# Two graph layers with a nearest-neighbour search: the squared norms of the search added by 32-row matmuls in four row groups

## The chip, the core and the metric

The kernel runs on one core of one Trainium2 chip. The metric is the device time of one execution in microseconds, the median of several runs.

## What is computed

Two graph layers act on `x` (4096 nodes of 128 features) with a dense weighted adjacency `adj` (4096 x 4096). The first layer builds node vectors `z`, finds for each node its four nearest neighbours by squared distance, and adds weights exp(-distance/2) for them to the adjacency. Cut to what matters:

```python
z  = leaky_relu(_lap_mul(A, x) @ W1 + b1, negative_slope=0.1)
sq = jnp.sum(z * z, axis=-1)
d2 = sq[:, None] + sq[None, :] - 2.0 * (z @ z.T)
S  = jnp.exp(-jnp.sqrt(jnp.maximum(d2, 0.0) + 1e-10) / (2.0 * sigma))
S  = jnp.where(ranks_of_S < 4, S, 0.0)
out = _lap_mul(S + A, x) @ W2 + b2
```

The second layer is a plain `x @ W_self.T + (adj @ x) @ W_neigh.T + b`. Both layers have a layer norm, a ReLU and a residual around them.

## The kernel before, in words

The program is written engine by engine, with semaphores by hand; each engine executes its own list in order. There are 32 tiles of 128 nodes (`TILES`), taken in 8 groups of 4 (`GROUPS`, `U`). Names on the left of `<-` in a row are what is written.

1. **Reading the adjacency** (0 to about 412 us). GpSimd issues the loads of `adj` (L365), VectorE transposes blocks of 32 (L862), ScalarE sums rows, and the transposed units go back to memory for later passes.
2. **First pass** (to about 541 us). TensorE multiplies stored units (L1157) group after group. When a group's product is complete, a chain `finish_first` of small steps turns it into z: VectorE `add_partial` (L908), TensorE L1204, VectorE `make_z` (L924 four times, L926), TensorE transposes (L1150) into the bank `ps_t`, ScalarE copies the part of z rounded to fp32r into `zt_hi` (L686) and squares it (L689), VectorE `split_z` writes the rest into `zt_lo` (L931), TensorE multiplies the squares by a matrix of -0.5 (L1217). This leaves in every row of the bank `ps_q` the same thing: minus half the squared norm of each of the group's 512 nodes. Then comes what the change touches. ScalarE copies rows 0 to 31 of `ps_q`, rounded, into `sq_rows` (L695), and rows 32 to 63, rounded, into `z_st` (L697); VectorE's `split_sq` subtracts the rounded value in rows 32 to 63 and writes the rest there (L937). So row 0 of `sq_rows` holds the high part and row 32 the low part, and `pick` (ones in rows 0 and 32, zeros elsewhere) adds the two. The lists `STAGE_A/B/C` and `MAKE_Z`, `SPLIT_SQ`, counted in tiles of the pass, set where each engine does these steps; on VectorE `split_sq` of one group stands directly ahead of `make_z` of the next.
3. **Search** (about 541 to 809 us). For each of 32 tiles, GpSimd copies the tile's columns into `zs_hi`, `zs_lo` (`stage_tile`, L492, L493); TensorE (`distances`) fills eight banks of 512 columns with four matmuls each: the norms (L1252) and the three products of high and low parts (L1253 to L1255); ScalarE (`leave`, L714) brings each pair of banks to `keys[par]`, one buffer for even tiles and one for odd. VectorE searches a pair of tiles: of the even tile only the maximum of each block of 128 (`bmax`, L975, then L977, L981), of the odd one all 4096 keys (MAX8 L988, FIND_INDEX8 L990), then the even tile's four best blocks, which GpSimd has fetched back from memory (`read_blocks`, L498 to L505), as candidates (L995, L997). `leave` of an even tile waits for `block_maxima` of the pair before and for the store of its keys (`keys_out`), of an odd one for `max_done` (L990). On GpSimd the staging of the odd tile stands behind the four fetches of `read_blocks`, and these wait for `block_places` (L981) and for `keys_out`. From tile 1 on, TensorE's matmul into an even bank waits until ScalarE has taken that pair of banks of the tile before (`key_ev`).
4. **Second and third pass** (about 809 us to the end): three matmuls per block (L1274 to L1276) over operands split on ScalarE (L731) and VectorE (L1018), with the gathers of the neighbours on GpSimd (L576) beside the second.

Of the kernel before, what the change touches and what calls it, by code (L numbers as in the profile page):

```python
# [22 lines left out]
F32 = mybir.dt.float32  # L23
# [12 lines left out]
U = 4  # L36
# [14 lines left out]
def gnn_kernel(nc, x, adj, W1, b1, W2, b2, W, b, out):  # L51
# [16 lines left out]
    with ctx:  # L68
# [538 lines left out]
        def _(act):  # L607
# [71 lines left out]
            def finish_first(k):  # L679
# [15 lines left out]
                act.activation(sq_rows_g[0:R, g], ps_q[0:R].rearrange("p (u q s) -> p u q s", u=U, q=QD), ACT.Copy).then_inc(qh_done, 1)  # L695
                act.wait_ge(sq_done, k + 1)
                act.activation(flat(z_st[R:2 * R]).bitcast(F32R), ps_q[R:2 * R], ACT.Copy).then_inc(qh_done, 1)  # L697
# [133 lines left out]
        def _(v):  # L831
# [11 lines left out]
            link(v.memset(pick[:].bitcast(F32), 0.0))  # L843
            v.memset(pick[0:1].bitcast(F32), 1.0)
            v.memset(pick[R:R + 1].bitcast(F32), 1.0)
            v.memset(sq_rows[2 * R:P].bitcast(F32), 0.0)
# [87 lines left out]
            def split_sq(k_f):  # L934
                g = F1[k_f]
                v.wait_ge(qh_done, 2 * k_f + 2)
                v.tensor_tensor(sq_rows_g[R:2 * R, g], ps_q[R:2 * R].rearrange("p (u q s) -> p u q s", u=U, q=QD),  # L937
                                z_st[R:2 * R].rearrange("p u (q s) -> p u q s", s=R), ALU.subtract).then_inc(q_done, 1)
# [198 lines left out]
        def _(pe):  # L1137
# [105 lines left out]
            def distances(it, par):  # L1243
                pe.wait_ge(zs_ready, it * 2 + 2)
                for c in range(8):
                    cols = slice(c * 512, c * 512 + 512)
                    if c % 2 == 0 and not (isinstance(it, int) and it < 1):
                        pe.wait_ge(key_ev, it * 4 + (c // 2 - 3))
                    zh = zt_hi[:].rearrange("p q t s -> p (q t s)")[:, cols]
                    zl = zt_lo[:].rearrange("p q t s -> p (q t s)")[:, cols]  # L1250
                    sq = sq_rows[:].rearrange("p q t s -> p (q t s)")[:, cols]
                    pe.matmul(ps[:, c], pick[:], sq, start=True, stop=False)  # L1252
                    pe.matmul(ps[:, c], zs_hi[:, par], zl, start=False, stop=False)  # L1253
                    pe.matmul(ps[:, c], zs_lo[:, par], zh, start=False, stop=False)  # L1254
                    ins = pe.matmul(ps[:, c], zs_hi[:, par], zh, start=False, stop=True)  # L1255
                    if c % 2:
                        ins.then_inc(bank_mm, 1)
# [110 lines left out]
```

## Time and profile before

| | us |
|---|---|
| median of 3 runs | 1305.23 |
| the three runs | 1304.32, 1305.23, 1310.51 |
| the profiled execution, its own time | 1303.21 |
| its span, first to last instruction | 1301.2 |

Mean granted TensorE clock over the span: 0.886 of full speed (full is 2.4 GHz, the lower level is half of it).

| stretch | us from the span's start |
|---|---|
| adjacency read and transposed | 0 to 412 |
| first pass | 412 to 541 |
| search | 541 to 809 |
| second and third pass | 809 to 1301 |

How to read it: a timeline row gives start, duration, engine, line, operation, what is written and read, the count, and in brackets the engine's idle time before it and what ended that. A matmul's row is longer than the distance to the next one's start, since matmuls are pipelined; the distance of two starts is what a matmul costs in a stream. PEld rows are weight loads.

### The profile page before, as it was taken

The numbers are of one execution on the slowest core, as the hardware profiler recorded it, in microseconds if no ns is written. First come the engines' busy times: TensorE is split into PE (matmuls) and PEld (weight loads), VectorE is DVE, ScalarE is ACT, GpSimd is POOL, SyncE is SP. The second block draws the span as 40 slices with busy tenths as digits, with TensorE's granted clock in tenths as the row PEclk, the third lists the DMA queues.
The fourth block names the chain that finished last, engine by engine and source line by source line (L and its number), as shares of the span: only waits on it lengthen the run. The fifth ranks groups of instructions, "written<-read, shape, count | busy, mean of one in ns | idle before, by whom it ended". The sixth has DMA issues, their size and how long they took to land.

```text
span 1301.2 us, 13552 instructions
## 1 busy us (share of the span) xinstructions
PE 934.7 (72%) x3570; PEld 664.9 (51%) x3570; DVE 888.0 (68%) x852; ACT 597.3 (46%) x1105; POOL 657.8 (51%) x936
## 2 busy tenths in 40 slices
PE   0132154474776999899999994666777777799998
PEld 0111022232333444477777773455666666588886
DVE  1966665654554321288999999937777777788885
ACT  0533343162460322255555555635555554567673
POOL 9798779877820000044444444588888887200000
PEclk9985676786987999899999998788888888899999
DMA  9999999999996975295444445695777777599993
GB/s 222 323 349 367 363 343 382 349 365 351 354 374 230 357 266 187 92 262 200 158 157 157 155 157 206 184 379 203 282 279 271 284 274 273 215 358 384 381 382 124
DMA packets 117253, 357.73 MB, mean 275 GB/s; under 512 B 34528, under 2 KB 59872, under 8 KB 89568
## 3 DMA queue, kind: packets, MB, share of 16 engines
q1 hardware_dynamic: 60896, 273.11, 55.2%
q0 software_dynamic: 47104, 80.00, 20.6%
q10 hardware_dynamic: 9216, 4.20, 1.2%
q8 instruction: 14, 0.23, 0.1%
q14 instruction: 23, 0.19, 0.0%
HBM read 250.02 MB, written 106.95 MB: 274 GB/s over the span
## 4 chain that ended last, share of the span: by engine, by line
PE 31%; POOL 21%; DMA 18%; issue 14%; DVE 11%; ACT 2%; SPq 1%; POOLq 0%; DVEq 0%; ACTq 0%
DMA araw<-in_adj_dram 15%; POOL zt_lo L576 11%; PE ps L1157 7%; POOL araw L365 7%; PE ps L1274 4%; PE ps L1275 4%; PE ps L1276 4%; PE ps L1252 2%; PE ps L1253 2%; PE ps L1254 2%; PE ps L1255 2%; DVE m L988 2%; DVE bmax L975 2%; DVE i L990 2%; POOL t_st L505 1%
## 5 line engine op out<-in xcount | busy, mean ns | idle before, releaser
L365 POOL DMA_DIRECT2D araw<-in_adj_dram x512 | 301.1, 597 | 66.4 <-ACTq L637 26.9
L1018 DVE TENSOR_TENSOR araw_r<-araw,tr_r 128x2048 fp32r<-128x2048 f32 x128 | 289.4, 2296 | 44.6 <-ACT tr_r L731 44.4
L731 ACT ACTIVATE tr_r<-araw 128x2048 fp32r<-128x2048 f32 x128 | 241.7, 1911 | 66.2 <-PE ps L1276 37.9
L576 POOL DMA_INDIRECT zt_lo<-neighbour_table,idx_st x128 | 193.9, 1515 | 45.7 <-issue 39.2
L714 ACT ACTIVATE araw<-ps,nsq 128x1024 f32<-128x1024 f32 x128 | 142.5, 1117 | 115.3 <-PE ps L1255 96.0
L1274 PE MATMUL ps<-araw_r,zt_hi 128*128 128x512 f32 x256 | 110.2, 430 | 93.2 <-DVE araw_r L1018 63.9
L633 ACT ACTIVATE ps<-araw 128x256 f32<-128x256 f32 x304 | 111.1, 365 | 59.4 <-DMA araw<-in_adj_dram 55.3
L886 DVE TENSOR_REDUCE part<-araw 128x16 f32<-128x4096 f32 x13 | 57.4, 4413 | 98.1 <-DMA araw<-in_adj_dram 98.1
L1252 PE MATMUL ps<-sq_rows,pick 128*128 128x512 f32 x256 | 102.3, 400 | 17.7 <-POOL zs_lo L493 10.8
L1274 PE MATMUL ps<-araw_r,ys_r 128*128 128x512 f32 x256 | 101.7, 397 | 9.5 <-DVE araw_r L1018 9.5
L1274 PEld LDWEIGHTS ps<-araw_r,zt_hi 128*128 128x128 f32 x256 | 52.1, 204 | 109.5 <-DVE araw_r L1018 69.4
L1275 PE MATMUL ps<-tr_r,sq_rows 128*128 128x512 f32 x256 | 105.9, 414 | 0.0
L1276 PE MATMUL ps<-tr_r,zt_hi 128*128 128x512 f32 x256 | 105.1, 411 | 0.0
L492 POOL CAST zs_hi<-zt_hi 128x128 fp32r (+1 forms) x32 | 9.4, 295 | 183.6 <-DVE zt_lo L931 166.8
L1253 PE MATMUL ps<-zt_lo,zs_hi 128*128 128x512 f32 x256 | 100.9, 394 | 0.0
L1254 PE MATMUL ps<-zt_hi,zs_lo 128*128 128x512 f32 x256 | 100.9, 394 | 0.0
L1157 PE MATMUL ps<-araw,ys 128*128 128x512 f32 x224 | 99.6, 593 | 1.8 <-DMA araw<-transposed 1.8
L1255 PE MATMUL ps<-zt_hi,zs_hi 128*128 128x512 f32 x256 | 100.7, 393 | 0.0
L1275 PE MATMUL ps<-tr_r,hs_r 128*128 128x512 f32 x256 | 100.6, 393 | 0.0
L1276 PE MATMUL ps<-tr_r,ys_r 128*128 128x512 f32 x256 | 100.5, 392 | 0.0
L1187 PE MATMUL ps<-part,fold 128*128 128x16 f32 x64 | 14.6, 367 | 118.6 <-DVE part L886 118.6
L862 DVE STREAM_TRANSPOSE tr<-araw 128x2048 f32<-128x2048 f32 x28 | 63.4, 2288 | 31.9 <-DMA araw<-in_adj_dram 31.8
(150 smaller groups left out, 1654.7 us busy)
## 6 DMA issues: line engine op xcount, KB each, us to landing
araw<-transposed SPq DMA_DIRECT2D x152, 1024.0 KB, 6.2
araw<-in_adj_dram POOLq DMA_DIRECT2D x512, 128.0 KB, 21.2
keys_scratch<-araw SPq DMA_DIRECT2D x64, 512.0 KB, 4.2
transposed<-tr SPq DMA_DIRECT2D x28, 1024.0 KB, 9.0
transposed<-unit_zt_hi SPq DMA_DIRECT2D x18, 1024.0 KB, 8.7
transposed<-unit_zt_lo SPq DMA_DIRECT2D x18, 1024.0 KB, 9.4
xs<-in_x_dram SPq DMA_DIRECT2D x64, 64.0 KB, 2.1
araw<-transposed SPq DMA_DIRECT2D x8, 512.0 KB, 7.4
```

The costliest lines, as they stand in the source:

```text
L365: gp.dma_start(araw[R * q + first:R * q + R:SPREAD, c], adj_v[q, first:R:SPREAD, g // 2, g % 2, :, c]).then_inc(a_first_in[c], DMA)
L576: gp.indirect_dma_start(out=gath[:, i, u, k, :], out_offset=None, in_=table, in_offset=bass.IndirectOffsetOnAxis(ap=idx_st[:, i, u * TOPK ...
L714: act.activation(keys[par][:, c * 1024:c * 1024 + 1024], ps[:, 2 * c:2 * c + 2].rearrange("p a b -> p (a b)"), ACT.Identity, bias=nsq[:, b ...
L731: act.activation(ring_hi[:, place % TSLOTS], ring[:, j], ACT.Copy).then_inc(hi_done, 1)
L1018: v.tensor_tensor(ring_lo[:, j], ring[:, j], ring_hi[:, place % TSLOTS].bitcast(F32), ALU.subtract).then_inc(lo_done, 1)
L1157: pe.matmul(acc[bank], ys[:, tile_at(c, place)], rhs(i, place), start=start and i == 0, stop=stop and i == len(tiles) - 1).then_inc(t_used, 1)
L1252: pe.matmul(ps[:, c], pick[:], sq, start=True, stop=False)
L1253: pe.matmul(ps[:, c], zs_hi[:, par], zl, start=False, stop=False)
L1254: pe.matmul(ps[:, c], zs_lo[:, par], zh, start=False, stop=False)
L1274: pe.matmul(acc[bank], hi[:, t], t_lo, start=place == 0 and i == 0, stop=False)
L1275: pe.matmul(acc[bank], lo[:, t], t_hi, start=False, stop=False)
L1276: ins = pe.matmul(acc[bank], hi[:, t], t_hi, start=False, stop=place == GROUPS - 1 and i == U - 1)
```

## The change

The sum of the norms is laid out anew in three places.

- `finish_first` on ScalarE writes all 128 rows of `ps_q` into `sq_rows`, scaled by column 0 of `fold`. `fold` holds a one where row modulo 32 equals the column, so the high part stands in rows 0, 32, 64 and 96, and zeros elsewhere. The second copy takes all 128 rows.
- `split_sq` on VectorE subtracts over 128 rows into `z_st`, waits for that, and adds the low part times column 1 of `fold` with four more instructions, which puts it in rows 1, 33, 65 and 97. Each group of 32 rows of `sq_rows` then holds both parts, and `pick` is all ones.
- `distances` on TensorE goes by halves of four banks. It first issues the four norm matmuls of the half, each from another group of 32 rows (`pick[32r:32r+32]`, `sq_rows[32r:32r+32]`) into its own bank, then the three products of each bank.

```diff
--- before.py
+++ after.py
@@ -692,9 +692,10 @@
                     ins = act.activation(junk[0][:, u * F:u * F + F], z_st[:, u], ACT.Square, accum_out=nsq[:, t:t + 1])
                 ins.then_inc(sq_done, 1)
                 act.wait_ge(q_mm, k + 1)
-                act.activation(sq_rows_g[0:R, g], ps_q[0:R].rearrange("p (u q s) -> p u q s", u=U, q=QD), ACT.Copy).then_inc(qh_done, 1)
+                act.activation(sq_rows_g[:, g], ps_q.rearrange("p (u q s) -> p u q s", u=U, q=QD), ACT.Identity, scale=fold[:, 0:1])\
+                    .then_inc(qh_done, 1)
                 act.wait_ge(sq_done, k + 1)
-                act.activation(flat(z_st[R:2 * R]).bitcast(F32R), ps_q[R:2 * R], ACT.Copy).then_inc(qh_done, 1)
+                act.activation(flat(z_st[:]).bitcast(F32R), ps_q, ACT.Copy).then_inc(qh_done, 1)
 
             for k in range(GROUPS):
                 finish_first(k)
@@ -840,10 +841,7 @@
             v.memset(ident[:], 0.0).then_inc(const_st, 1)
             v.memset(fold[:], 0.0).then_inc(const_st, 1)
             v.memset(neghalf[:], -0.5).then_inc(const_st, 1)
-            link(v.memset(pick[:].bitcast(F32), 0.0))
-            v.memset(pick[0:1].bitcast(F32), 1.0)
-            v.memset(pick[R:R + 1].bitcast(F32), 1.0)
-            v.memset(sq_rows[2 * R:P].bitcast(F32), 0.0)
+            v.memset(pick[:].bitcast(F32), 1.0)
             v.wait_ge(x_in, X_IN)
             for t in range(TILES):
                 ins = v.bn_stats(out=stats[:, t], in_=xs[:, t])
@@ -934,8 +932,11 @@
             def split_sq(k_f):
                 g = F1[k_f]
                 v.wait_ge(qh_done, 2 * k_f + 2)
-                v.tensor_tensor(sq_rows_g[R:2 * R, g], ps_q[R:2 * R].rearrange("p (u q s) -> p u q s", u=U, q=QD),
-                                z_st[R:2 * R].rearrange("p u (q s) -> p u q s", s=R), ALU.subtract).then_inc(q_done, 1)
+                link(v.tensor_tensor(flat(z_st[:]), ps_q, flat(z_st[:]), ALU.subtract))
+                for u in range(U):
+                    ins = v.scalar_tensor_tensor(sq_rows_g[:, g, u], z_st[:, u].rearrange("p (q s) -> p q s", s=R), fold[:, 1:2],
+                                                 sq_rows_g[:, g, u].bitcast(F32), ALU.mult, ALU.add)
+                ins.then_inc(q_done, 1)
 
             def stages(before, after):
 
@@ -1242,19 +1243,20 @@
 
             def distances(it, par):
                 pe.wait_ge(zs_ready, it * 2 + 2)
-                for c in range(8):
-                    cols = slice(c * 512, c * 512 + 512)
-                    if c % 2 == 0 and not (isinstance(it, int) and it < 1):
-                        pe.wait_ge(key_ev, it * 4 + (c // 2 - 3))
-                    zh = zt_hi[:].rearrange("p q t s -> p (q t s)")[:, cols]
-                    zl = zt_lo[:].rearrange("p q t s -> p (q t s)")[:, cols]
-                    sq = sq_rows[:].rearrange("p q t s -> p (q t s)")[:, cols]
-                    pe.matmul(ps[:, c], pick[:], sq, start=True, stop=False)
-                    pe.matmul(ps[:, c], zs_hi[:, par], zl, start=False, stop=False)
-                    pe.matmul(ps[:, c], zs_lo[:, par], zh, start=False, stop=False)
-                    ins = pe.matmul(ps[:, c], zs_hi[:, par], zh, start=False, stop=True)
-                    if c % 2:
-                        ins.then_inc(bank_mm, 1)
+                zh, zl, sq = [z[:].rearrange("p q t s -> p (q t s)") for z in (zt_hi, zt_lo, sq_rows)]
+                for half in range(2):
+                    for c in range(half * 4, half * 4 + 4):
+                        r, cols = c % 4, slice(c * 512, c * 512 + 512)
+                        if c % 2 == 0 and not (isinstance(it, int) and it < 1):
+                            pe.wait_ge(key_ev, it * 4 + (c // 2 - 3))
+                        pe.matmul(ps[:, c], pick[R * r:R * r + R], sq[R * r:R * r + R, cols], start=True, stop=False)
+                    for c in range(half * 4, half * 4 + 4):
+                        cols = slice(c * 512, c * 512 + 512)
+                        pe.matmul(ps[:, c], zs_hi[:, par], zl[:, cols], start=False, stop=False)
+                        pe.matmul(ps[:, c], zs_lo[:, par], zh[:, cols], start=False, stop=False)
+                        ins = pe.matmul(ps[:, c], zs_hi[:, par], zh[:, cols], start=False, stop=True)
+                        if c % 2:
+                            ins.then_inc(bank_mm, 1)
 
             pe.wait_ge(q_done, GROUPS)
             for par in range(2):
```

TensorE, the first half of tile 0 in `distances`, behind the last group's L1217. Before:

```order
L1252 MATMUL ps<-sq_rows,pick 128x512
L1253 MATMUL ps<-zt_lo,zs_hi 128x512
L1254 MATMUL ps<-zt_hi,zs_lo 128x512
L1255 MATMUL ps<-zt_hi,zs_hi 128x512
L1252 MATMUL ps<-sq_rows,pick 128x512
```

With the change:

```order
L1252 MATMUL ps<-sq_rows,pick 128x512 x4
L1255 MATMUL ps<-zt_lo,zs_hi 128x512
L1256 MATMUL ps<-zt_hi,zs_lo 128x512
L1257 MATMUL ps<-zt_hi,zs_hi 128x512
L1255 MATMUL ps<-zt_lo,zs_hi 128x512
```

The norm matmuls of banks 1 to 3 have moved ahead of bank 0's products; their number is the same, and the first of a half now stands behind the waits for both pairs of banks.

VectorE, from `split_z` of one group to `make_z` of the next, in the first pass. Before:

```order
L931 TENSOR_TENSOR zt_lo<-ps,zt_hi 128x4x4x32
L937 TENSOR_TENSOR sq_rows<-ps,z_st 32x4x4x32
L924 SCALAR_TENSOR_TENSOR z_st<-ps,dinv,bias 128x128 x4
L926 SCALAR_TENSOR_TENSOR z_st<-z_st 128x512
L908 TENSOR_TENSOR xs<-ps,xs 128x4x4x32
```

With the change:

```order
L929 TENSOR_TENSOR zt_lo<-ps,zt_hi 128x4x4x32
L935 TENSOR_TENSOR z_st<-ps,z_st 128x512
L937 SCALAR_TENSOR_TENSOR sq_rows<-z_st,fold,sq_rows 128x4x32 x4
L922 SCALAR_TENSOR_TENSOR z_st<-ps,dinv,bias 128x128 x4
L924 SCALAR_TENSOR_TENSOR z_st<-z_st 128x512
```

Four instructions more stand between the subtraction and `make_z`. (Lines behind L844 are two lower there.)

## Rows read from the trace of the kernel before

**Rows 1.** The page's busy time of each engine, share of the span, instructions

```profile
PE 934.7 (72%) x3570; PEld 664.9 (51%) x3570; DVE 888.0 (68%) x852; ACT 597.3 (46%) x1105; POOL 657.8 (51%) x936
```

**Rows 2.** Groups by line, 600 to 798 us: count, busy us, mean ns, idle before

```profile
L1252 PE MATMUL ps<-sq_rows,pick 128*128 128x512 f32 x199 | 78.7, 395 | 13.1 <-POOL zs_lo L493 8.2 <-ACT araw L714 4.9
...
L988 DVE MAX8 m<-araw 128x8 f32<-128x4096 f32 x12 | 53.2, 4430 | 3.6 <-ACT araw L714 3.1
```

**Rows 3.** Timeline of VectorE in the search, 590 to 675 us

```profile
593.19 4.43 DVE L988 MAX8 m<-araw 128x8 f32<-128x4096 f32 x1 [2.49 <-ACT araw L714]
...
624.77 4.43 DVE L988 MAX8 m<-araw 128x8 f32<-128x4096 f32 x1 [0.52 <-ACT araw L714]
...
650.76 4.40 DVE L975 TENSOR_REDUCE bmax<-araw 128x32 f32<-128x4096 f32 x1
...
656.36 4.43 DVE L988 MAX8 m<-araw 128x8 f32<-128x4096 f32 x1 [0.51 <-ACT araw L714]
...
666.76 4.40 DVE L975 TENSOR_REDUCE bmax<-araw 128x32 f32<-128x4096 f32 x1
...
671.95 4.43 DVE L988 MAX8 m<-araw 128x8 f32<-128x4096 f32 x1
```

**Rows 4.** Timeline, 662 to 671 us: staging, the odd tile's start, its last eviction

```profile
662.67 0.29 POOL L493 CAST zs_lo<-zt_lo 128x128 fp32r x1
...
663.10 0.49 PE L1252 MATMUL ps<-sq_rows,pick 128*128 128x512 f32 x1 [0.81 <-POOL zs_lo L493]
...
663.43 0.40 PE L1253 MATMUL ps<-zt_lo,zs_hi 128*128 128x512 f32 x1
...
663.66 0.39 PE L1254 MATMUL ps<-zt_hi,zs_lo 128*128 128x512 f32 x1
...
670.73 1.12 ACT L714 ACTIVATE araw<-ps,nsq 128x1024 f32<-128x1024 f32 x1 [0.70 <-PE ps L1255]
```

**Rows 5.** Timeline of TensorE: starts after idle stretches, and matmuls behind one

```profile
582.72 0.49 PE L1252 MATMUL ps<-sq_rows,pick 128*128 128x512 f32 x1 [2.62 <-POOL zs_lo L493]
...
584.12 0.63 PE L1253 MATMUL ps<-zt_lo,zs_hi 128*128 128x512 f32 x1
...
584.55 0.63 PE L1254 MATMUL ps<-zt_hi,zs_lo 128*128 128x512 f32 x1
...
615.92 0.49 PE L1252 MATMUL ps<-sq_rows,pick 128*128 128x512 f32 x1 [2.29 <-POOL zs_lo L493]
...
679.08 0.49 PE L1252 MATMUL ps<-sq_rows,pick 128*128 128x512 f32 x1 [1.20 <-POOL zs_lo L493]
```

**Rows 6.** Windows: busy time of PE, PEld, DVE, ACT, POOL, granted clock, DMA, GB/s

```profile
583.70:587.10 3.40, 3.40 (x9) 2.60 (x9) 3.30 (x5) 1.11 (x1) 1.14 (x6) 0.51 0.77 306
615.90:619.30 3.40, 3.38 (x15) 2.83 (x16) 3.30 (x5) 1.12 (x1) 0.89 (x3) 1.00 0.52 201
```

**Rows 7.** Timeline of the first pass, 432 to 446 us

```profile
432.86 1.13 DVE L924 SCALAR_TENSOR_TENSOR z_st<-ps,dinv,bias 128x128 f32<-128x128 f32 x4 [2.41 <-PE ps L1204]
...
442.70 0.68 DVE L937 TENSOR_TENSOR sq_rows<-ps,z_st 32x512 fp32r<-32x512 f32 x1 [5.43 <-ACT z_st L697]
...
443.50 1.13 DVE L924 SCALAR_TENSOR_TENSOR z_st<-ps,dinv,bias 128x128 f32<-128x128 f32 x4
...
444.66 0.69 DVE L926 SCALAR_TENSOR_TENSOR z_st<-z_st 128x512 f32<-128x512 f32 x1
...
445.60 0.60 PE L1150 MATMUL ps<-ident,z_st 128*128 128x128 f32 x4
```

**Rows 8.** Timeline of TensorE, the search's first matmul

```profile
541.15 0.79 PE L1252 MATMUL ps<-sq_rows,pick 128*128 128x512 f32 x1 [2.01 <-DVE sq_rows L937]
```

**Rows 9.** Timeline of the first pair of the search, VectorE and GpSimd

```profile
559.53 4.43 DVE L988 MAX8 m<-araw 128x8 f32<-128x4096 f32 x1 [5.51 <-ACT araw L714]
...
568.63 0.69 DVE L995 MAX8 m<-t_st 128x8 f32<-128x512 f32 x1
...
558.64 1.19 POOL L505 DMA_INDIRECT t_st<-keys_scratch,block_row  x1 [3.97 <-DMA keys_scratch<-araw]
```

## The prediction

> **What bounds the kernel now.** The page's busy times come first: TensorE is busy for 72% of the span and VectorE for 68% [rows 1], so neither is the bound by its share, and the search has to be read by itself. The groups of the search's stretch show TensorE's norm matmul with 13.1 us idle before it, and the idle time of VectorE's MAX8 that waits for ScalarE with only 3.1 us in twelve pairs of tiles [rows 2]. VectorE hardly waits. Its timeline gives the shortest period: from the block maxima (L975) to MAX8 5.19 us where nothing is waited for (666.76 to 671.95), from MAX8 to the next block maxima 10.40 us (656.36 to 666.76), together 15.59 us a pair [rows 3]. So the stage has a floor in VectorE, and a cheaper TensorE can win back only VectorE's waits.
>
> What are they? The chain of waits, followed back from MAX8, goes through TensorE every second pair. The block maxima of a pair (start 650.76) release GpSimd's four fetches, behind which the odd tile is staged (L493, 662.67); then that tile's 32 matmuls run from 663.10, its last eviction starts at 670.73, and MAX8 follows at 671.95 [rows 3, 4]. That is 21.19 us. VectorE alone would come from 650.76 to the same place in 15.59 + 5.19 = 20.78 us. The chain through TensorE is longer by 0.41 us once in two pairs, and it is paid as the waits of 0.52 and 0.51 us before MAX8 at 624.77 and 656.36 [rows 3]; there are six such waits in the stage. Before it stands the filling of the pipeline, with waits of 5.51 us [rows 9] and 2.49 us [rows 3].
>
> **TensorE's part, a tile.** Let s be what a tile's matmuls get shorter by. In a stream a matmul costs the distance of two starts, 0.23 us (663.43 to 663.66), though its row is 0.39 to 0.40 us long; the first after a stop costs 0.33 us (663.10 to 663.43) [rows 4]. So a weight load that nothing hides is worth about 0.10 us, and what is left in flight behind the last start about 0.17 us. A half of four banks now spends 4 x 0.23 = 0.92 us on its norms. No row shows 32-row matmuls, so bounds: if the four run wholly beside each other and nothing is paid at the ends, the half spends 0.23 us and s is 2 x 0.69 = 1.4 us. If they run one after another and both changes of shape wait for the array to empty and load anew (0.17 + 0.10 each), it spends 0.92 + 0.54 = 1.46 us, s = -1.1 us. I take the middle case by the nearest rows: they overlap, the starts of three lie 0.10 us apart (a weight load each), and one emptying of 0.17 us stays: 0.23 + 0.30 + 0.17 = 0.70 us, s = 2 x 0.22 = 0.4 us.
>
> Two rules of the Trainium skill pull this apart. TensorE: Matmul & The Clock Gate, in the part on packing small matmuls, gives 3.07 times the speed for four row groups at 512 columns; by that the four would take 0.92 / 3.07 = 0.30 us, an estimate, and s would be 1.2 us. TensorEngine Tiling (Array Packing), Key Properties, says that changing the tiling mode drains TensorE, which this kernel now does four times a tile. No row here shows either; the first would lead to the second rival, the second alone to the fourth.
>
> **What s is worth.** In the steady stage, only the 0.41 us of the chain: s = 0.4 takes it away, more takes nothing more. 6 x 0.41 = -2.5 us. In the filling, tiles 0 and 1 run back to back ahead of the first MAX8: 2s and some 0.2 us more, since the first halves run at the lower clock: -1.0 us. The wait of 2.49 us behind it ends at most 1 us earlier too: it goes back to the store of pair 0's keys, whose landing (558.64) starts the fetches that VectorE reads at 568.63 [rows 9], and that is a transfer among other transfers. I count -1.0 us for the filling in all, with 0 and -3 us as ends.
>
> **What the new layout adds.** ScalarE's two copies are no wider along a row than before; the subtraction (0.68 us on 32 rows [rows 7]) is as long along a row on 128; I take all three at their price of before. But VectorE gets four more instructions a group. Four such instructions of `make_z` take 1.16 us (443.50 to 444.66) [rows 7]; with the wait for the subtraction I count 1.2 us. Where it is paid:
> - Last group: the subtraction ends the chain that releases TensorE's first norm matmul at 541.15 [rows 8]. All of it on the path, +1.2 us.
> - Groups of 442 and 452 us: `make_z` starts right behind `split_sq` (442.70, 443.50), and z is ready at 444.66 + 0.69 = 445.35, only 0.25 us before TensorE's transposes at 445.60 [rows 7]. TensorE will now wait 1.2 - 0.25 = 0.95 us in the middle of its unbroken stream of L1157, twice: +1.9 us.
> - The other five: VectorE stands idle before the next `make_z`, 2.41 us at 432.86 [rows 7] and longer at the four others. That idle time is the cover; nothing, and up to 1.2 us each if it were gone.
> The memsets that fall away end long before VectorE's first work on `x` and are worth nothing. The norm matmul of a half's third bank now waits for the eviction of both pairs of banks at once; ScalarE has emptied them 2 us before in the steady stage (cover: the other half), nothing.
>
> Sum: -2.5 - 1.0 + 1.2 + 1.9 = -0.4 us. The profiled execution took 1303.2 us and the median of the three is 2.0 us above; the difference carries over, so **1304.8 us**. A measurement can tell about 0.5%, 6.5 us, from no change, and this is far inside.
>
> **Rivals.**
> 1. *The clock falls in every pair* (chance 0.18). TensorE's idle time before the odd tile is 1.20 us in a period of 679.08 - 663.10 = 15.98 us [rows 4, 5]. At 15.59 us it becomes 0.8 + 2s. The trace brackets what that does: behind 2.29 us idle at 615.92 the granted clock stays 1.00, behind 2.62 us at 582.72 it falls to 0.51 for 3.40 us, that is from 2.4 to 1.2 GHz, with starts 0.43 us apart (584.12, 584.55) [rows 5, 6]. With s = 1.2 the idle time is 3.2 us. The odd tile then loses 3.4 x 0.49 = 1.7 us and is 0.5 us longer than now, in seven passages of the chain +3.5 us in place of -2.5; with the filling (-1.5) and the new layout (+3.1) +5.1 us, **1310 us**. For it: the better the packing works, the longer the idle time. Against it: it needs s above 0.8, and a longer period shortens nothing else.
> 2. *The packing works and the clock holds* (0.12). The same s, filling -3.0: -2.5 - 3.0 + 3.1 = -2.4 us, **1303 us**.
> 3. *The groups run one after another at no further cost, so the change does nothing of what it says* (0.08). s = 0: +3.1 us, **1308 us**.
> 4. *Slower: the change of shape empties the array* (0.14). This decides from s = -0.35 on, where the chain alone adds 7 x 0.35 = 2.5 and the filling 1.0 to the 3.1. At s = -1.1 TensorE's pair of tiles takes 15.98 - 1.20 - 0.39 = 14.39, plus 0.23, plus 2.2 = 16.8 us and is the bound itself: 13 x 1.0 more, filling +2.5, layout +3.1, 1324 us. In the middle of it, at -0.7, **1315 us**. For it: four changes of shape a tile. Against it: as long as the four overlap, each change would have to cost over 0.4 us, where the rows give 0.27; it takes matmuls that run one after another as well.
>
> My forecast keeps 0.48, with s from 0 to 0.75; its own range is 1302 to 1308 us.
>
> **How the numbers follow.** Slower by over 6.5 us: nearly all of rival 4 and a third of rival 1, 0.19. Faster by over 6.5 us: even all waits taken away leave -2.5 - 3.0 - 2.4 + 3.1, about -4.8 us; only scatter reaches it, 0.04. The rest, 0.77, is no change. The range runs from 1300 (rival 2 and the filling at its best) to 1316 us (the middle of rival 4).
>
> **What would show it.** In the profile after: the distance from a half's first norm matmul to its first product, 0.7 us where four starts take 0.92 now; MAX8 without waits and a period near 15.6 us; TensorE's idle time before the odd tile near 1.6 us and the clock at 1.00; the transposes at about 446.6 us with a wait for `make_z`; the first norm matmul about 3 us later than 541.15. Wrong: idle times above 2.6 us followed by starts 0.43 us apart, or an odd tile longer than its 7.6 us from first start to last eviction.

## The result

| | before | with the change |
|---|---|---|
| median, us (12 runs each) | 1301.19 | 1313.84 |
| lowest and highest | 1297.41, 1310.51 | 1308.62, 1316.25 |
| span of the profiled execution | 1301.2 | 1311.1 |
| first norm matmul of the search, us | 541.15 | 545.12 |
| from there to the first MAX8 | 18.38 | 16.75 |
| first to third MAX8 | 33.66 | 33.91 |
| third to last (sixteenth) MAX8 | 205.13 | 214.43 |
| last MAX8 to the end | 502.9 | 500.9 |

The change makes the kernel slower: ratio 1.0076, 95% interval 1.0054 to 1.0098, where no change had been forecast (1304.8 us against 1305.2 before). The medians are 12.7 us apart; the ratio is worth 9.9 us. The two spans differ by 9.9 us, and the rows of the table add up to it: +4.0 ahead of the search (0.7 of them stand there early in the first pass, ahead of every place where TensorE waits for the new work: the `make_z` at 432.86 starts at 433.53 with the change), -1.6, +0.2, +9.3 and -2.0 behind it. The 9.3 us arise in the steady part of the search, in thirteen pairs of tiles.

The page's engine line, which answers to [rows 1], has hardly moved:

```profile
PE 932.9 (71%) x3570; PEld 635.0 (48%) x3570; DVE 893.6 (68%) x881; ACT 595.3 (45%) x1105; POOL 657.1 (50%) x936
```

The packing works. This is TensorE's timeline over the second half of tile 0 (start, duration, engine, line, operation, count):

```profile
550.43 0.50 PE L1252 MATMUL ps<-sq_rows,pick 32*128 32x512 f32 x4
...
550.86 0.50 PE L1255 MATMUL ps<-zt_lo,zs_hi 128*128 128x512 f32 x1
...
551.20 0.39 PE L1256 MATMUL ps<-zt_hi,zs_lo 128*128 128x512 f32 x1
...
553.49 0.39 PE L1257 MATMUL ps<-zt_hi,zs_hi 128*128 128x512 f32 x1
...
553.81 0.51 PE L1252 MATMUL ps<-sq_rows,pick 32*128 32x512 f32 x4
```

The four 32-row matmuls together last 0.50 us where one of 128 rows lasts 0.39, so they run beside each other. (In the kernel with the change, rows behind the new `split_sq`, and ScalarE's behind its new copy, have a line number one higher than before: L976 is L975, L989 is L988, L715 is L714.) The first product starts 0.43 us behind the first of them and its successor 0.34 us later; a half takes 553.81 - 550.43 = 3.38 us, where sixteen matmuls took 3.63 (16 starts 0.227 us apart). That is s = 0.5 us a tile.

What is lost is the clock. First the window over the steady search of the kernel before, then of the one with the change (stretch, length, busy time of PE, PEld, DVE, ACT, POOL, granted clock, DMA share, GB/s):

```profile
593.20:798.30 205.10, 190.70 (x827) 153.80 (x825) 195.76 (x130) 116.15 (x105) 89.35 (x192) 1.00 0.41 154
```

```profile
595.80:810.20 214.40, 189.78 (x825) 131.28 (x824) 195.72 (x130) 115.76 (x105) 89.49 (x192) 0.93 0.39 148
```

1.00 has become 0.93. VectorE's timeline with the change answers to [rows 3]:

```profile
621.74 4.40 DVE L976 TENSOR_REDUCE bmax<-araw 128x32 f32<-128x4096 f32 x1
...
629.45 4.43 DVE L989 MAX8 m<-araw 128x8 f32<-128x4096 f32 x1 [2.62 <-ACT araw L715]
...
639.85 4.40 DVE L976 TENSOR_REDUCE bmax<-araw 128x32 f32<-128x4096 f32 x1
...
645.00 4.43 DVE L989 MAX8 m<-araw 128x8 f32<-128x4096 f32 x1
...
663.30 4.43 DVE L989 MAX8 m<-araw 128x8 f32<-128x4096 f32 x1 [2.80 <-ACT araw L715]
...
695.71 4.43 DVE L989 MAX8 m<-araw 128x8 f32<-128x4096 f32 x1 [1.37 <-ACT araw L715]
```

MAX8 at 629.45 and 663.30 waits for ScalarE 2.62 and 2.80 us, where it was 0.52; in each second pair it does not wait at all. TensorE's timeline shows both ends of it, to be held against [rows 4, 5]:

```profile
618.52 0.91 PE L1252 MATMUL ps<-sq_rows,pick 32*128 32x512 f32 x4 [3.64 <-POOL zs_lo L493]
...
619.95 0.63 PE L1256 MATMUL ps<-zt_hi,zs_lo 128*128 128x512 f32 x1
...
620.38 0.63 PE L1257 MATMUL ps<-zt_hi,zs_hi 128*128 128x512 f32 x1
...
648.16 0.39 PE L1257 MATMUL ps<-zt_hi,zs_hi 128*128 128x512 f32 x1
...
652.18 0.91 PE L1252 MATMUL ps<-sq_rows,pick 32*128 32x512 f32 x4 [3.64 <-POOL zs_lo L493]
...
653.62 0.63 PE L1256 MATMUL ps<-zt_hi,zs_lo 128*128 128x512 f32 x1
```

Before the odd tiles at 618.52 and 652.18 TensorE has been idle for 3.64 us, and soon behind them the starts lie 0.43 us apart (619.95, 620.38), until about 625 us: the lower clock, 1.2 GHz. That tile's keys come late, MAX8 waits (629.45), and so the block maxima of the pair after stand 18.11 us behind their predecessor (621.74, 639.85) instead of 15.6. They release the staging of the odd tile after the next, so this one starts late (652.18), while TensorE has long done what it had (648.16): idle for 3.64 us again, and the clock falls again. The period of the loop is two pairs, 663.30 - 629.45 = 33.85 us against 31.6 before. From the third to the last MAX8 the six waits add up to 12.6 us where the six of before add up to 3.1; the difference, 9.5 us, covers the stage's 9.3.

The new layout costs what its instructions cost, in the rows that answer to [rows 7, 8]:

```profile
447.21 0.66 PE L1151 MATMUL ps<-ident,z_st 128*128 128x128 f32 x4 [0.78 <-DVE z_st L924]
...
457.40 0.65 PE L1151 MATMUL ps<-ident,z_st 128*128 128x128 f32 x4 [0.91 <-DVE z_st L924]
...
543.92 1.14 DVE L937 SCALAR_TENSOR_TENSOR sq_rows<-z_st,fold,sq_rows 128x128 fp32r<-128x128 f32 x4
...
545.12 0.80 PE L1252 MATMUL ps<-sq_rows,pick 32*128 32x512 f32 x4 [3.17 <-DVE sq_rows L937]
```

TensorE now waits 0.78 and 0.91 us for `make_z`, at 447.21 and 457.40, which are 1.61 and 2.74 us later than the same transposes before (445.60, 454.66); the last group's four new instructions start at 543.92 and the search 1.2 us behind them.

### The profile page after: what moved, and what is told of

Read it like the earlier page. It is cut to its first block, busy times and chain, and to the rows that moved or that the text cites. A ratio compares the mean times of both kernels' runs of the same rounds, so it can differ in the third digit from the quotient of the medians.

```text
span 1311.1 us, 13581 instructions
## 1 busy us (share of the span) xinstructions
PE 932.9 (71%) x3570; PEld 635.0 (48%) x3570; DVE 893.6 (68%) x881; ACT 595.3 (45%) x1105; POOL 657.1 (50%) x936
## 4 chain that ended last, share of the span: by engine, by line
PE 26%; POOL 14%; issue 12%; DVE 10%; ACT 2%; DMA 1%; POOLq 1%; DVEq 0%; ACTq 0%; SPq 0%
POOL zt_lo L576 11%; PE ps L1158 5%; PE ps L1276 4%; PE ps L1277 4%; PE ps L1278 4%; DVE i L991 3%; DVE bmax L976 2%; PE ps L1255 2%; DVE m L989 2%; PE ps L1256 2%; PE ps L1257 2%; POOL t_st L505 1%; ACT araw L715 1%; PE ps L1252 1%; PE ps L1146 1%
## 5 line engine op out<-in xcount | busy, mean ns | idle before, releaser
L715 ACT ACTIVATE araw<-ps,nsq 128x1024 f32<-128x1024 f32 x128 | 140.5, 1116 | 125.0 <-PE ps L1257 91.5
L1255 PE MATMUL ps<-zt_lo,zs_hi 128*128 128x512 f32 x256 | 113.8, 445 | 0.0
L1256 PE MATMUL ps<-zt_hi,zs_lo 128*128 128x512 f32 x256 | 106.3, 415 | 0.0
L1257 PE MATMUL ps<-zt_hi,zs_hi 128*128 128x512 f32 x256 | 105.3, 411 | 0.0
L989 DVE MAX8 m<-araw 128x8 f32<-128x4096 f32 x16 | 70.9, 4428 | 20.6 <-ACT araw L715 20.1
```

Of the source, the lines that this page charges most:

```text
L715: act.activation(keys[par][:, c * 1024:c * 1024 + 1024], ps[:, 2 * c:2 * c + 2].rearrange("p a b -> p (a b)"), ACT.Identity, bias=nsq[:, b ...
L1255: pe.matmul(ps[:, c], zs_hi[:, par], zl[:, cols], start=False, stop=False)
L1256: pe.matmul(ps[:, c], zs_lo[:, par], zh[:, cols], start=False, stop=False)
L1257: ins = pe.matmul(ps[:, c], zs_hi[:, par], zh[:, cols], start=False, stop=True)
```

## The experiments

Intervals in brackets are 95%, ratios against the kernel before on the same chip. "Search" is the distance from the first norm matmul to the last MAX8 in the profiled execution: 257.2 us before, 265.1 with the change.

**The layout alone.**

```diff
 # distances(): order and 128-row matmuls of before
-v.memset(pick[:], 1.0)
+v.memset(pick[:], 0.0); v.memset(pick[0:2], 1.0)
```

> The new layout of the squared norms alone (high parts in rows 0, 32, 64, 96, low parts one row below), while the search keeps the old order and 128-row norm matmuls, with ones in rows 0 and 1 of pick. If the idle stretch of TensorE is what costs the change its time: +3.3 us against before (1.2 at the last group, twice 0.95 in the first pass), the search from its first norm matmul to its last MAX8 within 1 us of the 257.2 us of before, granted clock 1.00 in its steady part, MAX8 waits near 0.5 us every second pair. If the layout itself disturbs the search (other rows read), the search is longer by several us.

Ratio 1.0007 [0.9984, 1.0030], search 256.3 us, clock 1.00, waits 0.52 to 0.56. The search is untouched; in the profile the first norm matmul stands where the change has it (545.07), and the 3.3 us expected in front of it can't be told in the total time: 1.0025 lies inside the interval, and so does 1.

**The order alone.**

```diff
-pe.matmul(ps[:, c], pick[R * r:R * r + R], sq[R * r:R * r + R, cols], start=True, stop=False)
+pe.matmul(ps[:, c], pick[:], sq[:, cols], start=True, stop=False)
```

> The new order alone: norm matmuls of a half first, behind the waits for both pairs of banks, but 128 rows each and the old layout. If the idle stretch is the cause: nothing, within 1.5 us of before, since the tile's 32 matmuls take the same 7.3 us. If the earlier waits for the banks hold TensorE up, as a rival says: odd tiles longer than 7.6 us from first start to last eviction, MAX8 waits over 0.6 us, the search several us longer.

Ratio 1.0024 [1.0001, 1.0048], search 257.5 us, waits 0.48 to 0.55, clock 1.00. In the profile the earlier waits for banks hold nothing up. The ratio is 3 us, twice what was expected at most, but its interval barely leaves 1 out.

**The idle stretch filled.**

```diff
 def distances(it, par):
+    if par and not isinstance(it, int):
+        pe.wait_ge(key_ev, it * 4 - 3)
+        for _ in range(6):
+            pe.matmul(ps[:, 0], pick[:], sq_rows[...][:, 0:512], start=True, stop=True)
     pe.wait_ge(zs_ready, it * 2 + 2)
```

> The changed kernel with six more 128-row matmuls (0.23 us each, their result is overwritten) before TensorE waits for the odd tile's staging: it fills 1.4 us of the idle stretch. If the idle stretch lets the clock fall, and the fall costs the time: granted clock 1.00 in the search's steady part, no MAX8 wait above 0.3 us after 630 us, pairs of 15.6 us, 8 to 12 us less than the changed kernel, so -1 to +1 us against before. If the 32-row matmuls as such lower the clock or the bound is elsewhere: the clock still falls, and the time is that of the changed kernel or up to 1 us a pair longer.

Ratio 0.9993 [0.9967, 1.0019], median 1298.86 us. The six matmuls on TensorE's timeline, and the window over the steady search:

```profile
595.46 1.52 PE L1250 MATMUL ps<-sq_rows,pick 128*128 128x512 f32 x6
...
597.22 0.58 PE L1258 MATMUL ps<-sq_rows,pick 32*128 32x512 f32 x4 [0.24 <-issue]
```

```profile
590.10:792.30 202.20, 195.01 (x904) 137.76 (x902) 195.75 (x131) 116.51 (x105) 90.59 (x194) 1.00 0.42 161
```

TensorE does more and the kernel is faster than with the change, by the two ratios 11 us: no MAX8 wait behind the first, clock 1.00, search 250.6 us. That shows the idle stretch as the cause, and that 32-row matmuls by themselves do not cost the time.

**Less work and no packing.** The norm matmuls are left out.

```diff
-pe.matmul(ps[:, c], pick[:], sq, start=True, stop=False)
-pe.matmul(ps[:, c], zs_hi[:, par], zl, start=False, stop=False)
+pe.matmul(ps[:, c], zs_hi[:, par], zl, start=True, stop=False)
```

> The kernel before with the 256 norm matmuls left out (the squared norms of the other nodes are not added, so other neighbours come out); no 32-row matmul anywhere, old layout. A tile has 24 matmuls, 5.5 us, and TensorE's idle time grows more than in the changed kernel. If idle time is the cause: starts 0.43 us apart behind idle stretches over 2.6 us, granted clock in the search below 0.95; the odd tile starts with 1.8 us in hand, so MAX8 waits under 1.5 us, and the time within 5 us of before. If the 32-row matmuls are what lowers the clock: granted clock 1.00 in the steady search, no waits, and about 5 us less than before.

Ratio 1.0017 [0.9989, 1.0045], search 256.5 us, clock 0.89 in the steady search. A quarter less work on TensorE gains nothing. Of its idle stretches:

```profile
624.44 0.49 PE L1252 MATMUL ps<-zt_lo,zs_hi 128*128 128x512 f32 x1 [1.57 <-POOL zs_lo L493]
...
641.47 0.79 PE L1252 MATMUL ps<-zt_lo,zs_hi 128*128 128x512 f32 x1 [5.10 <-POOL zs_lo L493]
...
657.04 0.49 PE L1252 MATMUL ps<-zt_lo,zs_hi 128*128 128x512 f32 x1 [2.46 <-POOL zs_lo L493]
```

Behind 1.57 and 2.46 us idle the clock held, behind 5.10 us (as behind 2.76 to 5.32 at ten other places) it fell. No 32-row matmul is needed.

**The same time a tile as packed, without packing.** Two of eight norm matmuls left out, 30 matmuls of 128 rows.

```diff
-pe.matmul(ps[:, c], pick[:], sq, start=True, stop=False)
+if c % 4 < 3:
+    pe.matmul(ps[:, c], pick[:], sq, start=True, stop=False)
```

> The kernel before with a quarter of the norm matmuls left out (banks 3 and 7 of every tile get no squared norms, so other neighbours come out): 30 matmuls of 128 rows a tile, 6.8 us, which is the packed kernel's 6.8 us without any 32-row matmul. If idle time of TensorE alone lets the clock fall: the same picture as the changed kernel, idle stretches of 3 to 4 us every second pair, each with starts 0.43 us apart behind it, MAX8 waits of 1.4 to 2.8 us, over 262 us from the first norm matmul to the last MAX8. If the 32-row matmuls have a part in it: after the filling of the pipeline the idle time settles under 2.4 us, clock 1.00, search at 250 to 253 us.

Ratio 1.0104 [1.0050, 1.0159], median 1316.68 us, search 268.9 us. VectorE's waits and an odd tile's start:

```profile
629.18 4.43 DVE L988 MAX8 m<-araw 128x8 f32<-128x4096 f32 x1 [2.75 <-ACT araw L714]
...
663.09 4.43 DVE L988 MAX8 m<-araw 128x8 f32<-128x4096 f32 x1 [2.86 <-ACT araw L714]
```

```profile
651.89 0.79 PE L1253 MATMUL ps<-sq_rows,pick 128*128 128x512 f32 x1 [3.64 <-POOL zs_lo L493]
```

The picture of the changed kernel down to the 3.64 us. So the loss comes with the shorter tile and needs no 32-row matmul. Not every shorter tile loses: with 24 matmuls the time was that of before.

**Does a first fall start the loop?** Filling matmuls in the second and third pair only, in the packed kernel (y2_kick) and in the one with 30 matmuls (w1_three_kick).

```diff
-    if par and not isinstance(it, int):
+    if par and isinstance(it, int) and it > 1:
...
+for it in range(6):
+    distances(it, it % 2)
+with pe.Fori(3, TILES // 2) as pair:
```

> The changed kernel with the six filling matmuls in the second and third pair of the search only (tiles 3 and 5), none in the thirteen pairs behind. My theory now is a loop that keeps itself going: one fall of the clock makes MAX8 wait, the wait lengthens the next pair but one, and TensorE's idle time there is again long enough for a fall; the first fall, at the filling of the pipeline, starts it. Then keeping that one away is enough: idle times near 1.6 us, clock 1.00, no MAX8 wait over 0.3 us to the end, 250 to 251 us from the first norm matmul to the last MAX8, and the time of the kernel with the filling matmuls everywhere. If every steady pair of the changed kernel is idle long enough by itself, as rival 1 of the prediction had it, the waits of 1.4 to 2.8 us come back in the pairs without filling and the search takes over 260 us.

Ratio 1.0077 [1.0054, 1.0100], search 266.2 us: my theory of a loop that needs a first fall has failed for the packed kernel. The two odd tiles with filling show no wait, and then, in the first pair without filling:

```profile
602.03 0.61 PE L1258 MATMUL ps<-sq_rows,pick 32*128 32x512 f32 x4 [1.83 <-POOL zs_lo L495]
...
603.07 0.63 PE L1262 MATMUL ps<-zt_hi,zs_lo 128*128 128x512 f32 x1
...
603.49 0.63 PE L1263 MATMUL ps<-zt_hi,zs_hi 128*128 128x512 f32 x1
```

1.83 us idle were enough, less than the 2.29 us that were harmless before [rows 5]. From there on the idle stretches are 3.2 to 3.7 us, and the loop runs as in the changed kernel.

> The kernel with 30 matmuls of 128 rows a tile (banks 3 and 7 without squared norms), with six filling matmuls in the second and third pair only, as in the packed kernel that fell into the loop all the same. If the loop has two states and 128-row matmuls need a first fall to enter the bad one: idle stretches near 1.7 us behind the filled pairs, no fall of the clock, no MAX8 waits, about 251 us from the first norm matmul to the last MAX8, 12 us or more under the same kernel without filling. If a stretch of 1.8 us at this place lets the clock fall whatever the matmuls are: the loop starts at the fourth pair as it did in the packed kernel, and the search takes over 262 us.

Ratio 0.9992 [0.9958, 1.0026], but its ten executions fall into two groups:

```
us (mean granted clock over the span)
1294.76 (0.888)  1299.21 (0.889)  1301.25 (0.886)  1301.93 (0.886)  1302.19 (0.885)  1302.79 (0.885)
1307.71 (0.874)  1311.48 (0.873)  1313.30 (0.872)  1313.61 (0.873)
```

Without filling the same matmuls gave 1311.66 to 1318.61 us at clocks of 0.870 to 0.873 in all four executions. The profiled execution was of the second group: it had fallen behind a first idle stretch of 2.50 us (583.22), which the filling had not closed. I read the two groups as with and without the loop; only the one with it was profiled, so it is argued and not shown that the loop of 128-row matmuls has to be started, and that without a start the kernel runs free of it.

**The wait taken out of the way.** GpSimd stages both tiles ahead of the fetches, in the packed kernel (x5_stage) and in the one before (x6_stage_before).

```diff
 stage_tile(pair * 2, 0)
-read_blocks(pair - 1)
 stage_tile(pair * 2 + 1, 1)
+read_blocks(pair - 1)
```

> The changed kernel with both tiles of a pair staged on GpSimd ahead of the four fetches, so that TensorE's odd tile no longer waits for them; nothing else. If the way from the block maxima over the fetches to the odd tile carries both the waits and the idle stretch: no idle time over 2.3 us on TensorE in the steady part (it is cut in pieces by the waits for banks), clock 1.00, no MAX8 wait, 250 us for the search, 8 to 12 us below the changed kernel. If the clock falls from the lower busy share alone, however it is cut: clock below 0.97 and MAX8 waits over 1 us stay.

> The kernel before with the same staging, no packing. TensorE's 14.4 to 14.6 us a pair are under VectorE's 15.6, so the six waits of 0.5 us and the one of 2.5 us should go: search 251 to 253 us, 4 to 6 us less than before in the search. If it reaches the same search time as the packed kernel with this staging, packing is worth only what the filling of the pipeline gives (1.6 us to the first MAX8).

Packed: ratio 0.9956 [0.9933, 0.9978], search 250.7 us. Not packed: 0.9943 [0.9921, 0.9966], search 252.2 us. In both, no MAX8 waits behind the first; the group of the unpacked one (12 of them from 600 to 795 us, idle before them 0.6 us in all):

```profile
L988 DVE MAX8 m<-araw 128x8 f32<-128x4096 f32 x12 | 53.1, 4428 | 0.6
```

But in the packed kernel the clock still fell in five steady pairs, behind idle stretches of 1.76 us:

```profile
622.03 0.61 PE L1252 MATMUL ps<-sq_rows,pick 32*128 32x512 f32 x4 [1.76 <-POOL zs_lo L493]
...
623.97 0.63 PE L1257 MATMUL ps<-zt_hi,zs_hi 128*128 128x512 f32 x1
...
624.40 0.63 PE L1255 MATMUL ps<-zt_lo,zs_hi 128*128 128x512 f32 x1
```

So this expectation came true for the waits and the search, and not for the clock: 0.95 in the steady part, where 1.00 was expected. The falls cost nothing here (no MAX8 wait, 250.7 us), since the odd tile no longer starts at the last moment; by the two ratios this kernel is 16 us faster than with the change, more than the 8 to 12 expected. With 30 matmuls of 128 rows and this staging the clock did not fall once in thirteen pairs:

> The same 30 matmuls of 128 rows a tile, with both tiles staged ahead of the fetches: one idle stretch of about 1.76 us a pair, as in the packed kernel with that staging, where the clock fell in five of the steady pairs. If idle time alone does it: falls in several pairs here too, clock near 0.95. If the 32-row matmuls have a part: no fall after the filling, clock 1.00. MAX8 waits stay at zero either way, search 250 to 251 us.

```profile
614.03 0.49 PE L1253 MATMUL ps<-sq_rows,pick 128*128 128x512 f32 x1 [1.67 <-POOL zs_lo L493]
...
614.36 0.40 PE L1254 MATMUL ps<-zt_lo,zs_hi 128*128 128x512 f32 x1
...
614.59 0.39 PE L1255 MATMUL ps<-zt_hi,zs_lo 128*128 128x512 f32 x1
```

```profile
586.60:788.70 202.10, 176.84 (x766) 142.33 (x764) 195.72 (x130) 112.25 (x106) 90.21 (x192) 1.00 0.42 161
```

Ratio 0.9972 [0.9946, 0.9998], search 253.0 us where 250 to 251 were expected; the time over is in the filling of the pipeline. The packed kernel seems to lose the clock more easily: five falls behind seven stretches of 1.75 to 1.80 us there, none behind thirteen of 1.63 to 1.68 us here, nor behind six of 2.28 to 2.55 us in this run, the kernel before, x1_layout, x2_halves and x4_nonorm. But that is not shown. The stretches here are 0.1 us shorter than those they are compared with, and below 2.6 us no two runs have the two kinds of tile behind stretches of the same length. Kernels with 128-row matmuls also fell behind 2.02 us in x1_layout and 2.50 us in w1_three_kick. In x1_layout the shorter stretch is followed by the low clock and the longer one is not:

```profile
585.71 0.49 PE L1254 MATMUL ps<-sq_rows,pick 128*128 128x512 f32 x1 [2.02 <-ACT araw L715]
...
587.33 0.63 PE L1256 MATMUL ps<-zt_hi,zs_lo 128*128 128x512 f32 x1
...
587.75 0.63 PE L1257 MATMUL ps<-zt_hi,zs_hi 128*128 128x512 f32 x1
...
618.92 0.49 PE L1254 MATMUL ps<-sq_rows,pick 128*128 128x512 f32 x1 [2.29 <-POOL zs_lo L493]
```

And in x5_stage the clock fell behind 1.76 us at 622.03 and held behind the same 1.76 us at 746.42. So the length of one stretch does not decide alone. What does, the place of the stretch in time for instance, is a rival to the 32-row matmuls that no run sets apart. Two runs ask what the 32-row matmuls' part could be.

**Filling with 32-row matmuls.**

```diff
 def distances(it, par):
+    if par and not isinstance(it, int):
+        pe.wait_ge(key_ev, it * 4 - 3)
+        pe.wait_ge(key_ev, it * 4 - 2)
+        for _ in range(6):
+            for r in range(4):
+                pe.matmul(ps[:, r], pick[R * r:R * r + R], sq_rows[R * r:R * r + R][...], start=True, stop=True)
     pe.wait_ge(zs_ready, it * 2 + 2)
```

> The changed kernel with the idle stretch filled by 32-row matmuls: six rounds of four, one in each row group and bank, before the odd tile, 1.4 to 2 us of work. If any matmul keeps the clock up: as with the six filling matmuls of 128 rows, clock 1.00, no MAX8 waits, search near 250.6 us, 8 to 12 us under the changed kernel. If 32-row matmuls count for little: the falls stay, with starts 0.43 us apart in the odd tiles and MAX8 waits over 1 us, search over 260 us.

Ratio 0.9989 [0.9966, 1.0013], search 252.8 us, clock 1.00 behind the filling of the pipeline. The 2 us over what was expected are one fall there and the wait behind it, 1.65 us at 592.93.

```profile
613.34 1.67 PE L1250 MATMUL ps<-sq_rows,pick 32*128 32x512 f32 x24
...
615.59 0.51 PE L1259 MATMUL ps<-sq_rows,pick 32*128 32x512 f32 x4 [0.58 <-POOL zs_lo L493]
```

24 of them in 1.67 us, on average 0.07 us each, keep the clock up in the steady pairs like 128-row ones.

**The norms behind the products of each half**, with both tiles staged early.

```diff
 # per half: the twelve products first (start=True on the first of a bank)
+ins = pe.matmul(ps[:, c], pick[R * r:R * r + R], sq[R * r:R * r + R, cols], start=False, stop=True)
```

> The packed kernel with both tiles staged ahead of the fetches, and in each half the four 32-row matmuls behind the twelve products, so that 128-row matmuls follow directly on an idle stretch. If the 32-row stretch behind the idle one is counted with it: no fall behind idle stretches of about 1.8 us, clock 1.00 in the steady part, where norms first gave 0.95 and five falls. If the changes of shape anywhere in the tile are what lowers it: falls in several steady pairs as before, clock near 0.95. MAX8 waits stay at zero either way and the time within 3 us of that kernel.

Ratio 0.9964 [0.9940, 0.9988], clock 0.96, again falls, behind five of the seven idle stretches of 1.85 to 1.90 us in the steady pairs:

```profile
661.59 0.49 PE L1252 MATMUL ps<-zt_lo,zs_hi 128*128 128x512 f32 x1 [1.88 <-POOL zs_lo L493]
...
662.47 0.63 PE L1252 MATMUL ps<-zt_lo,zs_hi 128*128 128x512 f32 x1
...
662.90 0.63 PE L1253 MATMUL ps<-zt_hi,zs_lo 128*128 128x512 f32 x1
```

So it isn't the 32-row stretch directly behind the idle one. Whether the changes of shape have a part at all stays open: here the 32-row matmuls stand directly ahead of the idle stretch, and these stretches are longer than the 1.63 to 1.68 us behind which 128-row matmuls held.

**The layout made cheaper**, with the six filling matmuls.

```diff
 # one rounding on ScalarE, one step on VectorE
-act.activation(sq_rows_g[:, g], ps_q, ACT.Identity, scale=fold[:, 0:1])
-link(v.tensor_tensor(flat(z_st[:]), ps_q, flat(z_st[:]), ALU.subtract))
-v.scalar_tensor_tensor(sq_rows, z_st, fold[:, 1:2], sq_rows, ALU.mult, ALU.add)      # four times
+v.scalar_tensor_tensor(sq_rows, z_st, fold[:, 1:2], ps_q, ALU.mult, ALU.subtract)    # four times
+pick = -(fold[:, 0:1] + fold[:, 1:2])
```

> The kernel with six filling matmuls everywhere, and a cheaper making of the layout: ScalarE rounds ps_q once instead of twice, and VectorE makes high and low rows in one step of four instructions, z_st times column 1 of fold minus ps_q, with minus ones in rows 0 and 1 of each 32 of pick. If the added work of the layout is on the path as the traces say (1.2 us at the last group, 0.95 us twice), it goes: the distance from the last add_partial (L908 in before) to the first norm matmul falls from 10.9 us to about 9.1, and the time is 3 to 5 us under the kernel with the filling matmuls. If the layout's work is hidden: the same time as that kernel.

Ratio 0.9954 [0.9938, 0.9971], median 1297.50 us. The last group's end:

```profile
542.19 1.12 DVE L937 SCALAR_TENSOR_TENSOR sq_rows<-z_st,fold,ps 128x128 fp32r<-128x128 f32 x4 [2.07 <-ACT z_st L698]
...
543.37 0.80 PE L1256 MATMUL ps<-sq_rows,pick 32*128 32x512 f32 x4 [1.84 <-DVE sq_rows L937]
```

From the last `add_partial` (533.77) the first norm matmul is 9.60 us away, 9.76 before and 10.93 with the change. The added work of the layout is gone from the path, so that part is shown; the 9.1 us expected were too low. By the ratios it is 5 us faster than the kernel with the filling matmuls alone (0.9993 [0.9967, 1.0019]), as expected, but the two intervals overlap, and what the profile shows accounts for 3.0 us at most: 1.33 here, and the two in-pass waits for `make_z`, 0.78 and 0.91 us, which are gone. Its own search took 254.0 us in the profiled execution, 3.4 us more than with the filling alone, with one fall of the clock in the filling of the pipeline and a wait of 1.75 us behind it (595.23).

**All together**, with the filling matmuls before the even tile.

> All that helped together: packed norm matmuls, the layout made in one step, both tiles staged ahead of the fetches, and six filling matmuls of 128 rows before the even tile, where this staging leaves TensorE idle. Search 250.5 us with no waits and clock 1.00 after the filling, first norm matmul 9.6 us behind the last add_partial. Against before: 6.6 us in the search and 0.2 us ahead of it, 0.994 to 0.995 in ratio; against the unpacked kernel with that staging 1.5 us at most, which these runs can hardly tell. A rival: the filling matmuls hold up the even tile, MAX8 waits come back, and it is slower than that one.

Ratio 0.9952 [0.9925, 0.9980], median 1294.95 us, search 251.3 us, no waits behind the first, clock 1.00. This and the kernel before with the staging alone (0.9943 [0.9921, 0.9966]) beat both kernels and can't be told apart. The staging is two lines.

## Why the prediction was wrong, point by point

Forecast was no change, 1304.8 us; the kernel is slower, by 9.9 us in the profiled executions and by the ratio, at a median of 1313.84 us. That this median lies in the range of 1300 to 1316 us is luck: the upper end came from the middle of rival 4, a change of shape that costs time, and that isn't what happened; a loss of over 6.5 us had a chance of 0.19. (The lower end counts the filling's best twice, since rival 2's 1303 us has the -3.0 in it already.)

- **The tile's saving.** Taken 0.4 us from bounds of -1.1 and 1.4; measured 0.5. A half spends 3.38 - 12 x 0.227 = 0.66 us on its norms where 0.70 was taken. The size is right and its parts are not: the four start within 0.01 us of each other, where 0.10 us apart was taken, and nearly all of it is paid at the ends: 0.43 us from the first norm matmul to the first product, 0.11 us more than a usual distance of starts behind that (550.86 to 551.20), and 0.09 us more ahead of the next norms (553.49 to 553.81). Of what the Trainium skill says in TensorE: Matmul & The Clock Gate, Part 3: Packing small matmuls, the trace bears out the speed by durations (0.50 us for four against 0.39 for one, 3.1 times), but not the estimate of 0.30 us a half that the prediction made with it. The drain that the Trainium skill's TensorEngine Tiling (Array Packing), Key Properties, names stands in no row by itself; a half spends 0.43 us more than one distance of starts on its four norms and two changes of shape, where the prediction's rows had 2 x 0.27 for the changes at worst.
- **The new layout.** Predicted 1.2 + 1.9 = 3.1 us at three named places; measured 3.3 us between the `make_z` at 432.86 and 433.53 and the first norm matmul (541.15 and 545.12), nearly all of it at these three places. Right in the profile; x1_layout could not show it in the total.
- **The filling.** Predicted -1.0, measured -1.6 + 0.2 = -1.4 us.
- **The steady stage, the step that failed.** Predicted -2.5, measured +9.3 us. I computed the idle time from a steady period, 0.8 + 2s, which is 1.6 us at s = 0.4 and 1.8 at the measured 0.5, held it against the bracket of 2.29 and 2.62 us, and concluded that rival 1 needed s above 0.8. Both sides of this comparison failed. First the bracket: in y2_kick, where the filling matmuls had kept the clock up in the pairs ahead, the idle time was 1.83 us, as computed, and the clock fell all the same. Then the idle time: once the clock has fallen, it is not that of a steady pair. A MAX8 that waits lengthens the stretch between two block maxima, and the idle stretch two pairs on takes in that wait. After the fall during the filling, which was in the trace of before, the kernel before came back to 2.29 us and the clock held; the packed one came to 3.64 us and it fell. I had both rows, 582.72 and 615.92, and read them as two samples of a threshold instead of one chain, in which the second came of the first. Last, the fall costs time only because the odd tile starts at the last moment: with both tiles staged early (x5_stage) the clock fell in five steady pairs and no MAX8 waited. The remark that a longer period shortens nothing else missed what counts: it lengthens the idle time.
- **Rival 1** was the right mechanism with a chance of 0.18 and a time of 1310 us, at a wrong condition. Its price per fall (1.7 us lost in the odd tile) was low: behind the start of an odd tile the clock stayed low until 3.3 us (686.04 to 689.3) to 6.5 us (751.06 to 757.6) later, and MAX8 waited 1.4 to 2.8 us.
- **The bracket for the clock** (holds at 2.29, falls at 2.62 us idle) was drawn from two rows and was too firm: other executions fell behind 2.02 and 2.50 and held behind 2.55 us with 128-row matmuls, and in the packed kernels 1.76 and 1.83 us were enough, though not each time.

## What to carry to other kernels

An engine that is not the bound but stands in a chain that ends at the last moment can lose time by being made faster: here half a microsecond less work a tile cost the clock and 9.3 us, 1.8 us less work a tile (x4_nonorm) gained nothing, and two exchanged lines on GpSimd gained 0.57%. When a profile shows a fall of the clock that the kernel recovers from, ask what the recovery hangs on, and follow the wait that the fall causes to the next idle stretch; a shorter piece of work there can turn one fall into one in every period. Filling an idle stretch with matmuls whose result is thrown away is a cheap test of this cause.

## What the runs showed of the hardware

Four matmuls of 32 rows in four row groups and banks take 0.50 us where one of 128 rows takes 0.39, but the first product starts 0.43 us behind the first of the four, since they stand between matmuls of 128 rows; in a row of 24 the starts are on average 0.07 us apart. With 128-row matmuls the clock fell behind every idle stretch of 2.62 us and more that was read in the search, held behind most of 1.6 to 2.55 us, and fell once behind 2.02 and once behind 2.50 us; between tiles with packed norms it fell behind 1.76, 1.83 and 1.88 us, though not each time. Since below 2.6 us the lengths of the two kinds do not meet, this is no proof of a difference between them, and no run tells what decides. One program (w1_three_kick) had executions of two kinds, which I take for runs without and with a loop of falls that keeps itself going, though only one of the second kind was profiled: 1294.8 to 1302.8 us at a mean clock of 0.885 and more, or 1307.7 to 1313.6 us at 0.874 and less.
